# Normalised rows and softmax weights turned by DMAs, PV in three fp16 passes, the FFN over two steps

## The reference

```python
x = x + xattn(layernorm(x), ctx, ctx, mask)      # x [4, 2048, 512], ctx [4, 77, 512], 16 heads of 32
x = x + ffn(layernorm(x))

def xattn(q_src, k_src, v_src, mask):
    q, k, v = q_src @ Wq.T, k_src @ Wk.T, v_src @ Wv.T
    logits = einsum('bhqd,bhkd->bhqk', q, k) / sqrt(32);  logits = where(mask == 0, -1e9, logits)
    return (softmax(logits) @ v, heads joined) @ Wo.T

def ffn(x):                                       # M = 64 units, each with an inner layer of 16
    s = x @ Win + bin_
    h = relu(s[..., None] * W1 + b1)
    g = einsum('btmh,mh->btm', h, W2) + b2
    return g @ Wout + bout
```

## Time and profile before

| | |
|---|---|
| Time, median of 3 runs | 977.67 us (976.68 to 978.26) |
| Profiled execution, span from first to last instruction | 976.4 us |
| PE busy | 890.4 us (91%) |
| DVE busy | 743.7 us (76%) |
| ACT busy | 529.9 us (54%) |
| POOL busy | 445.5 us (46%) |

### The profile page before, as it was taken

How to read it: one execution, slowest core, us unless ns; L and a number is a source line. 1 busy time by engine, 2 the same in 40 slices (tenths; PEclk the granted TensorE clock), 3 DMA queues, 4 the chain that set the end, 5 groups by cost and what they waited for, 6 DMA issues and landing times.

```text
span 976.4 us, 15372 instructions
## 1 busy us (share of the span) xinstructions
PE 890.4 (91%) x5202; PEld 478.6 (49%) x5202; DVE 743.7 (76%) x1338; ACT 529.9 (54%) x897; POOL 445.5 (46%) x398
## 2 busy tenths in 40 slices
PE   6878799999999989999999989999999999997866
PEld 4434545454555545454555545454555545453331
DVE  2446888888979796888979786888979798778351
ACT  2334638475574837475574827475574738273622
POOL 4033445364636453364646453364645454455220
PEclk9799899999999999999999999999999999999997
DMA  9300000202020110202020110202020100001001
GB/s 341 96 1 0 13 1 7 88 1 87 7 74 21 61 33 4 87 1 87 7 87 8 65 30 3 87 1 87 7 88 7 66 21 35 10 1 44 4 40 44
DMA packets 23314, 42.77 MB, mean 44 GB/s; under 512 B 11519, under 2 KB 12183, under 8 KB 23231
## 3 DMA queue, kind: packets, MB, share of 16 engines
q1 hardware_dynamic: 22303, 40.44, 12.4%
q10 hardware_dynamic: 928, 1.27, 0.4%
HBM read 22.90 MB, written 16.78 MB: 41 GB/s over the span
## 4 chain that ended last, share of the span: by engine, by line
PE 60%; DVE 18%; issue 9%; ACT 7%; POOL 5%; ACTq 0%; DVEq 0%; POOLq 0%
PE mm_banks L1054 19%; PE tr_banks L1105 12%; PE lg_banks L1094 8%; PE mm_banks L1116 7%; DVE normed L862 4%; PE mm_banks L1159 3%; ACT inner L618 3%; DVE xr L846 3%; PE tr_banks L1063 3%; PE mm_banks L1170 3%; DVE row_sum L833 2%; PE tr_banks L1151 2%; DVE stats L787 2%; ACT pT L603 2%; PE tr_banks L1136 2%
## 5 line engine op out<-in xcount | busy, mean ns | idle before, releaser
L468 POOL TENSOR_TENSOR probs<-probs,row_max 128x616 f32<-128x616 f32 x128 | 154.4, 1217 | 181.8 <-DVE row_max L825 181.0
L475 POOL TENSOR_TENSOR probs<-probs,row_inv 128x616 f32<-128x616 f32 x128 | 156.6, 1224 | 154.9 <-DVE row_inv L835 154.9
L1054 PE MATMUL mm_banks<-xT,wqT 128*128 128x512 f16 x768 | 177.4, 382 | 1.5 <-DVE xT L800 1.5
L1054 PE MATMUL mm_banks<-woT,aT 128*128 128x512 f16 x768 | 168.4, 379 | 2.1 <-issue 2.1
L1105 PE MATMUL tr_banks<-ident,probs 128*77 128x128 f32 x1024 | 155.7, 282 | 15.0 <-ACT inner L618 6.1
L1105 PEld LDWEIGHTS tr_banks<-ident,probs 128*77 128x77 f32 x1024 | 117.5, 148 | 95.1 <-issue 34.5
L603 ACT ACTIVATE pT<-tr_banks 77x512 f32<-77x512 f32 x256 | 145.7, 589 | 20.5 <-PE tr_banks L1105 18.2
L1094 PE MATMUL lg_banks<-k_blocks,qT 128*128 128x308 f16 x768 | 125.2, 300 | 15.4 <-issue 12.6
L833 DVE TENSOR_REDUCE row_sum<-probs 128x8 f32<-128x616 f32 x128 | 100.3, 784 | 46.2 <-ACT probs L598 45.2
L586 ACT ACTIVATE hT<-tr_banks 128x512 f16<-128x512 f32 x64 | 34.8, 594 | 171.5 <-PE tr_banks L1136 171.5
L1054 PEld LDWEIGHTS mm_banks<-woT,aT 128*128 128x128 f16 x768 | 75.1, 98 | 93.3 <-issue 3.2
(11 more groups left out here) (80 smaller groups left out, 1055.5 us busy)
## 6 DMA issues: line engine op xcount, KB each, us to landing
xr<-in_x SPq DMA_DIRECT2D x32, 512.0 KB, 4.6
out_x<-xr SPq DMA_DIRECT2D x32, 512.0 KB, 2.8
k_blocks<-kT_all SPq DMA_DIRECT2D x32, 38.5 KB, 2.2
probs<-in_L_xattn_Wk SPq DMA_DIRECT2D x1, 1024.0 KB, 8.7
probs<-in_L_xattn_Wq SPq DMA_DIRECT2D x1, 1024.0 KB, 12.8
probs<-in_L_xattn_Wv SPq DMA_DIRECT2D x1, 1024.0 KB, 14.4
probs<-in_L_xattn_Wo SPq DMA_DIRECT2D x1, 1024.0 KB, 16.2
xr<-in_ctx SPq DMA_DIRECT2D x1, 616.0 KB
```

The lines of the kernel that those rows point to most:

```text
L468: pool.tensor_tensor(block_of(g, k), block_of(g, k), top, ALU.subtract).then_inc(shifted, 1)
L475: pool.tensor_tensor(block_of(g, k), block_of(g, k), inv, ALU.mult).then_inc(probs_ready, 1)
L1054: last = pe.matmul(bank, stationary(a, c), moving(b, c), start=(n == 0), stop=(n == len(passes) - 1))
```

## The change

1. **Rows turned by DMAs.** `x_normal` and now also `h_normal` run on ScalarE into buffers of two tiles. ScalarE copies them to the high part, GpSimd (`x_low`) or VectorE (`h_low`) forms the low part, both in SBUF. SyncE then turns both parts of a tile with one `dma_start_transpose` (`turn_x`, `turn_h`: 128 rows by 1024 fp16 columns, 256 KB, eight 128x128 blocks). The TensorE transposes are gone.
2. **Softmax weights turned by DMAs.** `divide` now also multiplies by 4096. ScalarE writes the high part (`p_part`), GpSimd the low part (`p_low`), and SyncE turns a half (`turn_p`: 128 rows by 2048 fp16 columns, 512 KB, sixteen blocks, each head padded from 77 to 128 columns). `probs` holds four halves instead of sixteen, so `maxima` of a half waits for `p_low` of the half four before it. `p_parts` holds two halves. `p_transposes` and `p_copies` are gone. `sums` works on tiles (two halves), with one more small scaling instruction.
3. **PV in three fp16 passes** (`pv`, twelve matmuls for four heads instead of four fp32 ones). `v` is kept in two parts.
4. **The FFN over two steps.** `ffn_in` (now twelve matmuls of 64 columns of weights, in pairs on the two halves of the bank), `s_part`, `s_low`, and `ffn_pre` and `relus` 0 to 3 are done at the end of the step of BACK. The FFN part of the next step does `ffn_g` in two halves, `ffn_pre` and `relus` 4 to 7, `ffn_out` and `output`. `add_bout` is gone, and a third matmul in `ffn_out` adds the output bias.
5. **Orders.** All five engines have new orders. The weights `wv` and `wo` are prepared at the end of step 0, in one piece.

The diff, cut to its core:

```diff
+P_SCALE = 4096.0
+PS = 2
+IN_SLOTS = 4
...
-    [(FRONT, "xT", k) for k in range(0, 2)] + [(BACK, "pT", k) for k in range(0, 2)] + [(FFN, "pre", 0)]
-    + [(BACK, "pT", 2)] + [(FFN, "pre", 1)] + [(BACK, "pT", k) for k in range(3, 5)]
-    + [(FFN, "pre", k) for k in range(2, 4)] + [(BACK, "pT", 5)] + [(FFN, "pre", k) for k in range(4, 6)]
-    + [(BACK, "pT", 6)] + [(FFN, "pre", k) for k in range(6, 8)] + [(BACK, "pT", 7)] + [(FRONT, "xT", 2)]
-    + [(LATE, "wvT", k) for k in range(0, 4)] + [(BACK, "pT", k) for k in range(8, 12)] + [(FRONT, "xT", 3)]
-    + [(BACK, "pT", k) for k in range(12, 15)] + [(LATE, "woT", k) for k in range(0, 2)] + [(BACK, "pT", 15)]
-    + [(LATE, "woT", k) for k in range(2, 4)] + [(BACK, "hT", k) for k in range(0, 4)]
+    [(FFN, "pre", k) for k in range(4, 8)] + [(FRONT, "q", k) for k in range(0, 3)]
+    + [(BACK, "pre", k) for k in range(0, 2)] + [(FRONT, "q", 3)] + [(BACK, "pre", k) for k in range(2, 4)]
+    + [(LATE, "wvT", k) for k in range(0, 4)] + [(LATE, "woT", k) for k in range(0, 4)]
-    [(FFN, "s", 0)] + [(BACK, "pv", 0)] + [(FFN, "g", 0)] + [(BACK, "pv", 1)]
-    + [(FFN, "out", k) for k in range(0, 3)] + [(LATE, "v", k) for k in range(0, 2)] + [(FFN, "out", 3)]
-    + [(BACK, "pv", 2)] + [(FRONT, "q", 0)] + [(LATE, "v", k) for k in range(2, 4)] + [(FRONT, "q", 1)]
-    + [(BACK, "pv", 3)] + [(FRONT, "q", 2)] + [(BACK, "wo", k) for k in range(0, 4)] + [(FRONT, "q", 3)]
+MM_ORDER = (
+    [(FFN, "g", 0)] + [(BACK, "pv", k) for k in range(0, 4)] + [(FFN, "out", k) for k in range(0, 4)]
+    + [(BACK, "wo", k) for k in range(0, 4)] + [(BACK, "s", 0)] + [(LATE, "v", k) for k in range(0, 4)]
...
+            def turn_x(step, t):
+                if t == 0 and not step.first(-1):
+                    tr.wait_ready(sp, step.before(), "q", C - 1)
+                sp.wait_ge(x_lowered, T * step.group(1).n + t + 1)
+                sp.dma_start_transpose(xT[:, t, :, :, :].rearrange("p a c r -> p (a c) r"),
+                                       x_parts[:, t, :, :].rearrange("p a d -> p (a d)")).then_inc(x_turned[t], 16)
+
+            def turn_h(step, t):
+                if t == 0 and not step.first(1):
+                    mm.wait_ready(sp, step.before(), "s", 0)
+                sp.wait_ge(h_lowered, T * step.group(-1).n + t + 1)
+                sp.dma_start_transpose(hT[:, t, :, :, :].rearrange("p a c r -> p (a c) r"),
+                                       h_parts[:, t, :, :].rearrange("p a d -> p (a d)")).then_inc(h_turned[t], 16)
+
+            def turn_p(step, k):
+                g, k, n = half_of(step, k)
+                if k == 0 and n > 0:
+                    mm.wait_ready(sp, step, "pv", C - 1)
+                if k == 0 and n == 0:
+                    sp.wait_ge(wout_placed, 2 * 16 * J)
+                sp.wait_ge(p_lowered, n + 1)
+                t, u = k // 2, k % 2
+                sp.dma_start_transpose(pT[:, u, :, :, P * t:P * (t + 1)].rearrange("p a h r -> p (a h) r"),
+                                       p_parts[:, k % PS, :, :, :].rearrange("p a h k -> p (a h k)"))\
+                    .then_inc(p_turned[k % PS], 16)
...
+                if back:
+                    turn_p(step, -4)
+                    turn_p(step, -3)
+                    turn_p(step, -2)
+                    turn_p(step, -1)
+                if front:
+                    for t in range(T):
...
+                if ffn:
+                    store(step, 0)
+                if soft:
+                    turn_p(step, 0)
+                if ffn:
+                    store(step, 1)
+                if soft:
+                    turn_p(step, 1)
+                if ahead and ffn:
+                    reload(step, 0)
+                    reload(step, 1)
+                if back:
+                    turn_h(step, 0)
+                if soft:
+                    turn_p(step, 2)
+                if back:
+                    turn_h(step, 1)
+                if soft:
+                    turn_p(step, 3)
+                if back:
+                    turn_h(step, 2)
+                    turn_h(step, 3)
...
-            def add_bout(step, t):
-
-                g = step.group(-1)
-                if step.first(1) and t == 0:
-                    pool.wait_ge(bout_loaded, 16)
-                pool.wait_ge(h_norm, 4 * g.n + t + 1)
-                h = xr[:, g.slot, t, :]
-                pool.tensor_tensor(h, h, bout_rows[:, :], ALU.add).then_inc(bout_added, 1)
+            def x_low(step, t):
+                pool.wait_ge(x_high, T * step.group(2).n + t + 1)
+                pool.tensor_tensor(x_parts[:, t, 1, :], x_normed[:, t % 2, :], x_parts[:, t, 0, :], ALU.subtract)\
+                    .then_inc(x_lowered, 1)
+            def divide(step, k):
+                g, k, n = half_of(step, k)
+
+                pool.wait_ge(inv_done, T * g.n + k // 2 + 1)
+                inv = row_inv[:, k // 2, k % 2, :].unsqueeze(2).broadcast_to([P, 2 * HC, KEYS])
+                pool.tensor_tensor(block_of(k), block_of(k), inv, ALU.mult).then_inc(probs_ready, 1)
+
+            def p_low(step, k):
+                g, k, n = half_of(step, k)
+
+                pool.wait_ge(p_high, n + 1)
+                pool.tensor_tensor(p_parts[:, k % PS, 1, :, 0:KEYS], block_of(k), p_parts[:, k % PS, 0, :, 0:KEYS],
+                                   ALU.subtract).then_inc(p_lowered, 1)
...
-            def p_copies(step, *heads):
-                for h in heads:
-                    tr.wait_ready(act, step, "pT", h)
-                    tr.read(act.activation(pT[0:KEYS, h % 8, :], tr.bank(step, "pT", h)[0:KEYS, :], ACT.Copy),
-                            step, "pT", h)
+            def p_part(step, k):
+                g, k, n = half_of(step, k)
+                if not (isinstance(n, int) and n < PS):
+                    act.wait_ge(p_turned[k % PS], 16 * (HALVES // PS * g.n + k // PS))
+                act.wait_ge(probs_ready, n + 1)
+                act.activation(p_parts[:, k % PS, 0, :, 0:KEYS], probs[:, k % 4, :].rearrange(
+                    "p (h k) -> p h k", k=KEYS), ACT.Copy).then_inc(p_high, 1)
+            def relus(step, *chunks):
+                for j in chunks:
+                    tr.wait_ready(act, step, "pre", j)
+                    if j >= IN_SLOTS:
+                        act.wait_ge(g_taken, step.group(-2).n + 1)
+                    elif FFN in step.parts:
+                        mm.wait_ready(act, step, "g", 0)
+                    tr.read(act.activation(inner[:, j % IN_SLOTS, :], tr.bank(step, "pre", j), ACT.Relu,
+                                           bias=inner_cols[:, 1, j:j + 1], scale=w1_div[:, j:j + 1]), step, "pre", j)
...
-            def h_normal(step, t):
-                g = step.group(-1)
-                dve.wait_ge(h_rstd, 2 * g.n + t // 2 + 1)
-                dve.tensor_scalar(normed[:, t, :], xr[:, g.slot, t, :], mean_var[:, 1, t, 0:1], rstd[:, 1, t:t + 1],
-                                  ALU.subtract, ALU.mult).then_inc(h_norm, 1)
+                if not (isinstance(n, int) and n < 4):
+                    dve.wait_ge(p_lowered, n - 3)
+            def sums(step, tile):
+                n = T * step.i + tile
+                g = step.group(0) if tile >= 0 else step.group(-1)
+                tile = tile % T
+                for u in range(2):
+                    k = 2 * tile + u
+                    dve.wait_ge(exp_done, 2 * n + u + 1)
+                    dve.tensor_reduce(row_sum[:, 0, u, :], probs[:, k % 4, :].rearrange("p (h k) -> p h k", k=KEYS),
+                                      AX.X, ALU.add).then_inc(sum_done, 1)
+                dve.wait_ge(sum_done, 2 * n + 2)
+                dve.tensor_scalar(row_sum[:, 1, :, :], row_sum[:, 0, :, :], 1.0 / P_SCALE, None, ALU.mult)\
+                    .then_inc(scaled, 1)
+                dve.wait_ge(scaled, n + 1)
+                dve.reciprocal(row_inv[:, tile, :, :], row_sum[:, 1, :, :]).then_inc(inv_done, 1)
+            def h_low(step, t):
+                dve.wait_ge(h_high, T * step.group(-1).n + t + 1)
+                dve.tensor_tensor(h_parts[:, t, 1, :], h_normed[:, t % 2, :], h_parts[:, t, 0, :], ALU.subtract)\
+                    .then_inc(h_lowered, 1)
...
-                for h in range(HC):
-                    last = pe.matmul(mm.bank(step, "pv", c)[DK * h:DK * (h + 1), :],
-                                     v_now[:, DK * (HC * c + h):DK * (HC * c + h + 1)], pT[0:KEYS, (HC * c + h) % 8, :],
-                                     start=True, stop=True)
+            def pv(step, c):
+                g = step.group(-1)
+                if c == 0:
+                    for s in range(PS):
+                        pe.wait_ge(p_turned[s], 16 * (HALVES // PS) * (g.n + 1))
+                    if step.v % 4 == 1:
+                        pe.wait_ge(v_ready, 16 * (step.t + step.v // 4 + 1))
+                mm.wait_free(pe, step, "pv", c)
+                for m, (vp, pp) in enumerate(((0, 0), (0, 1), (1, 0))):
```

(49 more changed lines are left out.)

794 lines of the change are left out of this document (356 added, 438 removed).

## The result

| | before | after |
|---|---|---|
| median (range) | 977.96 us (976.68 to 982.23) | 1379.84 us (1375.65 to 1381.16), 4 runs |
| ratio | | 1.4078, 95% interval 1.4032 to 1.4123 |
| span of the profiled execution | 976.4 us | 1378.3 us |
| one step | 53.6 us | 78.9 us |

What follows compares the result with a forecast made beforehand. PE bounded the kernel before; after the change a closed path through the queues would: 61.8 + 10.4 landings + 6 clock = 78 us a step; 130 + 1170 + 50 + 12 = 1362 us, range 1170 to 1760.

Steps and rivals of the forecast that it cites:

- The round: Closed path of one step through the engines' queues, from `h_low` 3 to the next: 61.8 us without DMAs, 78 in all.
- The signs: Expected in the trace: Q matmuls 70 to 85 us apart, PE near half busy, gaps of 4 to 10 us.
- A and B, 27.7 us: A: `turn_h` 3 landed to `s_part` ended, 2.2 us; B: from `s_part` to `p_low` -1, 25.5 us.
- C, 34.1 us: From `pv` through Wo and residual to `h_low` 3: 34.1 us, of which 30 are VectorE's own work.
- The clock term of 6: PE at granted clock 0.50 after waits before `ffn_in` and `pv`: 6 us more per step, from 0 to 10.
- PV: The four column groups overlap, so PV's three passes take 0.65 us for four heads, 2.6 in all.
- The landings, 10.4 us: Turning DMAs on the path: 4.6 us for `turn_p` -1 and 5.8 after `h_low` 3, together 10.4 per step.
- `turn_p` 3 and `turn_h` 2, 1 MB in all: Transfers in front of `turn_h` 3, taken to need 8.7 us from the end of `p_low` 3 (31.2 of C, 34.1 us).
- Around the steps: Outside the rounds: 130 us before the first `pv`, 50 for the last group and FFN half, 12 for loop turns.
- turning DMAs are slow: Rival, chance 0.22: SyncE's turning DMAs at 16.2 us per MB take 102 us per step, 1722 us in all.
- prompt turns, warm clock: Rival, chance 0.18: both landings 2.2 us and no loss of clock give a step of 66.2, 1185 us.

Runs made afterwards that it cites:

- the cut order: Changed kernel with the softmax tail (blocks 4 to 7) moved from the next step into its own, ahead of or between the `relus`: 1188.95 us.
- the run with idle matmuls at both places: Kernel with the softmax tail moved ahead of the FFN, plus 40 useless matmuls before `pv` and 24 before `ffn_in`: 1289.73 us.
- small `p_low`: `p_low` computed for 77 of 616 columns: 1314.84 us on the changed kernel, 1166.37 us with the softmax tail ahead of the FFN.
- three further orders by hand: Softmax-tail-first kernel with `logits` 3 and `wo` 0 earlier: 1197.61 us; changed kernel in two orders written anew: 1296.26 and 1333.11 us.

## Why the prediction was right

1362 us was predicted, 1380 measured, by the mechanism named as the likeliest. Its steps against the rows:

- *The round.* Shown: the chain after is that path, and the run that cuts it at the place in ScalarE's queue that the prediction named, with the moves on GpSimd and VectorE that go with it, gives back 191 of 402 us with all the work in place, of which some 45 at most may belong to the moved `x_normal` and `x_part`. The gap before `pv` went with it.
- *The signs.* PE waits 10.0 us before `pv` and 5.8 before `ffn_in`, as predicted; it is busy for 68% of the step, not for near half, since cold matmuls last longer.
- *A and B, 27.7 us.* From 737.55 (hT landed) to 768.50 (`p_low` -1 ended) it took 31.0. The cold stretches are more than the difference: `ffn_in` 2.79 for 1.3 and Q's last bank 5.31 for 2.6 are 4.2 us, which the sum had under the clock. `p_low` was priced at 1.5 and took 1.32.
- *C, 34.1 us.* It took 39.5 (694.48 to 733.97), the largest error of a term. PV was cold (5.65 us in PE's timeline, where 2.6 was predicted), and so were the four `ffn_out` and the first Wo bank (3.79 for 2.59). The last Wo bank ended 26.5 us after `pv` began, where 22 was predicted: 4.5 of the 5.4 are there. VectorE, which was to show no long gap in C, waited 3.9 us for `logits` 3, which stands behind them. The clock term of 6 was thus somewhat small: with the 4.2 of A and B it is up to 8.7.
- *PV.* The prediction takes the x8 of a PV bank for eight matmuls. It is four: the trace has two records for each fp32 matmul (512 in all, for 16 groups of 16 heads). Its conclusion holds: twelve fp16 matmuls in four column groups took 0.79 us warm in the run with idle matmuls at both places, near the predicted 0.65 and far from the 2.6 that they would take one after another.
- *The landings, 10.4 us.* pT took 4.86 from the end of `p_low` -1 to `pv` (4.6 predicted), hT 3.6 from the end of `h_low` 3 (5.8 predicted). The step that was mis-sized is "`turn_p` 3 and `turn_h` 2, 1 MB in all", at 8.7: `p_low` 3 ended at 730.79 and the last of this 1 MB landed 6.8 us later. The two errors, 2 us too much for the landings and 2.7 too little for C and the clock, nearly cancel: 61.8 + 10.4 + 6 = 78.2 against 78.9. That the step came out within 1 us is in part luck.
- *Around the steps.* First `pv` at 143.65 (130 predicted), fifteen rounds in 1174.6 us (1182 with the loop's turns), 60.0 behind the last `pv` (50). These 24 us, less 7, are the difference of 16 us between the predicted time and the span. Two of the fifteen rounds, not three, hold a turn of the loop (83.8 and 84.0 us, 5 more than their neighbours), and the first and the last two are shorter than 78.
- *The rival "turning DMAs are slow".* Shown wrong: as plain copies they give back 41 us. On the Trainium skill (VectorE: DVE Perf Modes, The three transpose paths), its 1309 ns for a 128x128 block by DMA is no rate: a `turn_p` holds sixteen such blocks and lands in 4.4 us. The Trainium skill's other page (Advanced Engine Details and Errata, X-Bar Transpose), by which a turning DMA is about as fast as a plain one, agrees with these landings, 4.4 against 4.2, and 2.8 against 2.3 for 256 KB. The 350 to 400 GB/s of the same section of the Trainium skill weren't reached: with the DMA engines full, the windows of hT's last transfers show 210.
- *The rival "prompt turns, warm clock", 1185 us.* Neither of its conditions was met by a run. The plain copies (1339) landed in 4.2 us for pT and not in 2.2, and with the idle matmuls (1322) part of the round stayed cold. The two weren't run together in this order.

What stays open is the rest, 211 us between the cut order (1189) and the kernel before. Its chain shows a new round of 66.6 us, and no run cuts that one. The small `p_low` (22.6 us) and the plain copies (13.5) show that no single one of these parts sets the step there, and three further orders by hand ended at 1198, 1296 and 1333. A third buffer for `p_parts`, for whose two `p_part` 6 and 7 wait, wasn't tried, nor more than four blocks of `probs`. Whether an order of this work near 978 exists wasn't shown either way; no version here beats the kernel before.

## What to carry to other kernels

When work is taken from the engine that bounds a kernel and given to transfers and splits on the others, add up the path that leads through all in-order queues from one step to the same place in the next, before adding up loads: here every engine's busy time in a step lay below the old step of 53.6 us, and the step grew by 25 us. A part's price depends on the order: idle matmuls, plain copies and a smaller `p_low` won 58, 41 and 65 us in one order; in the other the idle matmuls lost 101, and the two others won 13.5 and 22.6. To find such a round, look in the chain for one step that returns to its own start through every engine, and cut it where a queue puts late work of one half in front of ready work of the other; then read the waits again, since a moved instruction makes new ones.
